# Self-attention's first projections moved into the last groups of cross-attention, in a fused Perceiver layer

## What is computed

```python
def cross(q_in, ctx):                          # x normed, ctx 32 x 256 x 256
    q, k, v = heads16(q_in @ Wq), heads16(ctx @ Wk), heads16(ctx @ Wv)
    return merge(softmax(q @ k.T) @ v) @ Wo
def self_attn(x):                              # x normed
    q, k, v = x @ wq.T, x @ wk.T, x @ wv.T     # per head, 1024 columns in all
    return merge(softmax(causal(q @ k.T / 8)) @ v) @ wo.T
def ffn(x):
    W_in, W_out = quantize_w8(W_in), quantize_w8(W_out)
    h = gelu(quantize_a16(x) @ W_in + b_in)    # a16: scale from the largest |x| of the whole tensor
    return quantize_a16(h) @ W_out + b_out
x = x + cross(norm(x), ctx)
x = x + self_attn(norm(x))
x = x + ffn(norm(x))
```

## Time and profile before

| what | us |
|---|---|
| median of 3 runs | 645.09 |
| their span | 645.08 to 646.16 |
| the profiled execution | 644.6 |
| its span, first to last instruction | 642.9 |
| PE busy | 599.8 (93%) |
| DVE busy | 470.9 (73%) |
| ACT busy | 383.6 (60%) |
| POOL busy | 163.4 (25%) |

### The profile page before, as it was taken

How to read it: one execution, slowest core, us unless ns; L and a number is a source line. 1 busy time by engine, 2 the same in 40 slices (tenths; PEclk the granted TensorE clock), 3 DMA queues, 4 the chain that set the end, 5 groups by cost and what they waited for, 6 DMA issues and landing times. The chain is left out here.

```text
span 642.9 us, 18565 instructions
## 1 busy us (share of the span) xinstructions
PE 599.8 (93%) x6777; PEld 514.1 (80%) x6777; DVE 470.9 (73%) x978; ACT 383.6 (60%) x1012; POOL 163.4 (25%) x229
## 2 busy tenths in 40 slices
PE   6599999999999999889898999999999999799897
PEld 4588888888888898768697989898989898644597
DVE  4478788888888887768799666666666656677797
ACT  3488788888888888756332333333333333457784
POOL 6524233324342423000211212121212111260400
PEclk9899999999999999999999999999999999999999
DMA  6997867686767767814000000000000000000012
GB/s 197 268 259 183 190 162 182 167 191 168 183 171 185 171 162 206 244 54 140 2 2 2 2 0 0 0 0 0 0 0 0 3 1 2 3 2 0 0 50 83
DMA packets 37037, 58.44 MB, mean 91 GB/s; under 512 B 6912, under 2 KB 15232, under 8 KB 36992
## 3 DMA queue, kind: packets, MB, share of 16 engines
q1 hardware_dynamic: 29328, 42.75, 26.2%
q10 hardware_dynamic: 4592, 8.78, 4.7%
q0 software_dynamic: 3072, 6.30, 4.0%
HBM read 17.96 MB, written 2.10 MB: 31 GB/s over the span
## 5 line engine op out<-in xcount | busy, mean ns | idle before, releaser
L624 ACT ACTIVATE Pr<-pS,nmax 128x256 f32<-128x256 f32 x256 | 120.0, 484 | 27.7 <-DVE nmax L732 27.7
L732 DVE TENSOR_REDUCE nmax<-pS 128x2 f32<-128x512 f32 x128 | 87.4, 684 | 20.2 <-PE pS L468 18.6
L478 PE MATMUL pT<-ident,Pr 128*128 128x128 f32 x512 | 78.1, 275 | 3.3 <-DVE wraw L737 3.1
L966 POOL TENSOR_TENSOR a_Pr<-a_Pr,a_rinv 128x512 f32<-128x512 f32 x32 | 32.7, 1043 | 185.8 <-DVE a_rinv L1277 185.8
L468 PE MATMUL pS<-Kst,Qst 96*128 96x256 f32 x256 | 58.9, 312 | 12.1 <-DMA Qst<-QSl 6.8
L1147 ACT ACTIVATE a_Pr<-a_Pr 128x512 f32<-128x512 f32 x32 | 20.2, 631 | 76.0 <-DVE a_Pr L1269 76.0
L478 PEld LDWEIGHTS pT<-ident,Pr 128*128 128x128 f32 x512 | 59.6, 141 | 4.6 <-issue 4.2
L468 PEld LDWEIGHTS pS<-Kst,Qst 96*128 96x128 f32 x256 | 40.2, 193 | 20.9 <-issue 10.0
L624 ACT ACTIVATION_READ_ACCUMULATOR Pr<-pS,nmax 128x1 f32 x256 | 55.0, 215 | 0.0
L287 POOL DMA_DIRECT2D Qst<-QSh x60 | 30.2, 506 | 80.5 <-PE pS L468 56.3
L59 PE MATMUL a_pJ<-a_XTh,a_W1h 128*128 128x256 f32 x128 | 37.1, 290 | 2.5 <-DVE X L1290 1.6
(11 more groups left out here) (323 smaller groups left out, 1974.6 us busy)
## 6 DMA issues: line engine op xcount, KB each, us to landing
Kst<-WO_ints SPq DMA_DIRECT2D x96, 128.0 KB, 3.1
CT<-ctxT ACTq DMA_DIRECT2D x16, 512.0 KB, 4.8
Kst<-KSh SPq DMA_DIRECT2D x62, 128.0 KB, 3.1
Qst<-QSh SPq DMA_DIRECT2D x64, 64.0 KB, 2.3
Qst<-QSh POOLq DMA_DIRECT2D x64, 64.0 KB, 2.9
Kst<-KSl SPq DMA_DIRECT2D x31, 128.0 KB, 3.3
Qst<-QSl SPq DMA_DIRECT2D x32, 64.0 KB, 2.2
Qst<-QSl POOLq DMA_DIRECT2D x32, 64.0 KB, 2.9
```

What stands on the lines that cost most here:

```text
L478: last = pe.transpose(pT[s % 2][:, t, k, :], Pr[s % 2][:, t, P * k:P * k + P], ident[:, :])
L624: act.activation(Pr[c % 2][:, t, :], pS[c % 2][:, t, :], ACT.Exp, bias=nmax[c % 2][:, t:t + 1], accum_out=rsum[par][:, c // 4, 2 * (c % 4) ...
L732: dve.tensor_reduce(nmax[s % 2][:, :], pS[s % 2][:, :, :], AX.X, ALU.max, negate=True).then_inc(maxed, 1)
L966: pool.tensor_tensor(rows, rows, rinv[s][:, :].unsqueeze(2).to_broadcast([P, 8, SQ]), ALU.mult).then_inc(weighted, 1)
```

## The change

- The head of self-attention goes. Quad 0's norm is made in cross-attention's group 6 (steps 4 and 8), its transposes, Q and K in group 7 by the fills of a new table `LAST`: X, the two V fills (now steps 2 and 3), four SQ fills (Q), four SK fills (K), of which the last stands after the group. The filler matmuls at cross-attention's end and in the head go too.
- The weights' splits go from ACT and DVE to POOL (`split_high`, `split_low`, in halves of 128x1024), after its last restack; that of `wo`'s low part (one instruction of 128x2048) to the start of POOL's list in self-attention.
- The split weights, Q and K of quad 0 and all later quads lie in buffers that cross-attention has done with (class `Shared`), K in `raw`. `w_out` gets a buffer of its own; W_in's turned integers and the biases lie in `raw`.
- SP loads `awq` at the end of group 5, `awk` in the middle of group 6.
- Head of cross-attention: the third context load is issued three fills later, and POOL issues the first restack of Q before `rstd_of(1)`.
- The loops over cross-attention's groups and self-attention's quads are written out.
- Feed-forward: the transposes go from block 1 to block 3, their evictions from block 2 to block 4.

```diff
+        self.W = [[cs[0], ks], [qs, cs[1]], [quarter[:2], quarter[2:]]]
+        self.QT = [ct[j // 4][:, 256 * (j % 4):256 * (j % 4) + 256] for j in range(HP)]
+        self.KT = [raw[:, 0, 256 * j:256 * j + 256] for j in range(HP)]
...
+        LAST = {0: ("X", 2, 0), 2: ("V", 1, 0), 3: ("V", 1, 1), 4: ("SQ", 2, 0), 6: ("SQ", 2, 1), 7: ("SQ", 2, 2),
+                8: ("SQ", 2, 3), 10: ("SK", 2, 0), 12: ("SK", 2, 1), 14: ("SK", 2, 2), 16: ("SK", 2, 3)}
...
-            body(0, False)
-            with eng.Fori(1, QUADS - 2) as i:
-                body(i, False)
-            body(QUADS - 2, False)
-            body(QUADS - 1, True)
+            for i in range(QUADS):
+                body(i, i == QUADS - 1)
...
+            def split_high(m):
+                pool.wait_ge(raw_in[m], 16)
+                for k in range(KC):
+                    pool.tensor_copy(shared.W[m][HI][k], raw[:, m, HE * k:HE * k + HE]).then_inc(weights_high, 1)
...
             steps(pool, body)
+            pool.wait_ge(proj, BEFORE_LAST)
+            split_high(0)
+            pool.wait_ge(kst_in[0], RESTACK * QUADS)
+            split_low(0)
+            for par in range(2):
+                q_restacked(pool, par, QUADS)
+            apart(pool, waited)
+            split_high(1)
+            pool.wait_ge(proj, BEFORE_LAST + 3)
+            split_low(1)
+            pool.wait_ge(scores, CHUNKS * (PAIRS - 1))
+            split_high(2)
+            split_low(2)
+            pool.wait_ge(raw_in[3], 16)
+            pool.tensor_copy(shared.WO_high, raw[:, 3, :])
...
+                elif kind in ("SQ", "SK"):
+                    m = ("SQ", "SK").index(kind)
+                    pe.wait_ge(lo, BEFORE_LAST + 1)
+                    pe.wait_ge(weights_split, m + 1)
...
             weigh(QUADS - 1, 12, True)
-            keep_busy(pe, 5, pJ[0][:, :], identb, causal)
+            r, k, kind, ahead, part = event(QUADS - 1, 16, True)
+            project(r, pJ[k % 2], r - 1, kind, part, PAIRS, 0)
             turn_o(PAIRS - 1)
-            keep_busy(pe, 3, pJ[0][:, :], identb, causal)
             turn_back(PAIRS - 1)
-            keep_busy(pe, 5, pJ[0][:, :], identb, causal)
             project_out(PAIRS - 1)
...
-            rstd_of(0)
             rstd_of(1)
+            flat = "p j d -> p (j d)"
+            pool.tensor_tensor(WO[LO].rearrange(flat), raw[:, 3, :], f32(WO[HI]).rearrange(flat), ALU.subtract
+                               ).then_inc(wo_split, 1)
...
-                    if f == 1 and not last:
+                    if f == 3 and not last:
                         turn(g + 1)
```

More of the change, by code:

```diff
@@ L250, in event @@
         def event(i, c, last):
+            if last:
+                if c not in LAST:
+                    return None
+                k = list(LAST).index(c)
+                return BEFORE_LAST + k, k, *LAST[c]
             if c not in EVENTS:
@@ L449, in project @@
                     last = split_matmul(pe, bank[:, :], weights(1, slice(P * part, P * part + P)), parts(CS[b]))
+                elif kind in ("SQ", "SK"):
+                    m = ("SQ", "SK").index(kind)
+                    pe.wait_ge(lo, BEFORE_LAST + 1)
+                    pe.wait_ge(weights_split, m + 1)
+                    for t in range(2):
+                        j = 2 * part + t
+                        last = split_matmul(pe, bank[:, 256 * t:256 * t + 256], shared.weights(m, slice(P * j, P * j + P)),
+                                            parts(XT))
                 else:
@@ L691, in _ @@
             take_even(PAIRS - 1)
+            r, k, kind, ahead, part = event(QUADS - 1, 16, True)
+            high(r, pJ[k % 2], kind, ahead, part, QUADS - 1)
             o_high(PAIRS - 1)
@@ L829, in _ @@
             merge(PAIRS - 1)
+            r, k, kind, ahead, part = event(QUADS - 1, 16, True)
+            low(r, pJ[k % 2], kind, ahead, part, QUADS - 1)
             scale_o(PAIRS - 1)
@@ L994, in bank_read @@
                 if kind == "X":
-                    pe.wait_ge(xt_lo, 2 * quad + part + 1)
+                    pe.wait_ge(xt_lo, 2 * (quad - 1) + part + 1)
                 elif kind == "Y":
@@ L1001, in bank_read @@
                     done, order = (by_act, BY_ACT) if (kind, part) in BY_ACT else (by_dve, BY_DVE)
-                    pe.wait_ge(done, len(order) * quad + order.index((kind, part)) + 1)
+                    pe.wait_ge(done, len(order) * quad + order.index((kind, part)) + 1 - AHEAD)
             def fill(bank, kind, part, quad):
@@ L1047, in score @@
                             rows, side = slice(E * h2, E * h2 + E), (h2 + b) % 2
-                            last = pe.matmul(out[b][SQ * side:SQ * side + SQ, j, :], QT[rows, j, tok],
-                                             KT[rows, j, tok], start=False, stop=True, skip_group_check=True)
+                            last = pe.matmul(out[b][SQ * side:SQ * side + SQ, j, :], QT[j][rows, tok],
+                                             KT[j][rows, tok], start=False, stop=True, skip_group_check=True)
                 last.then_inc(scored, 2)
@@ L1691, in hidden @@
                                       apply_absolute_value=True).then_inc(h_max, 1)
-                    if f == 2 and not last:
+                    if f == 4 and not last:
                         x_low(g + 1)
```

225 lines of the change are left out of this document (111 added, 114 removed).

## The result

| what | before | after |
|---|---|---|
| median of 4 runs, us | 645.62 | 639.73 |
| their span | 645.08 to 646.25 | 635.43 to 641.30 |
| the profiled execution | 644.6 | 641.3 |
| its span | 642.9 | 639.4 |

The ratio is 0.9895, with a 95% interval of 0.9873 to 0.9916: 6 us faster, where 9 were forecast. The profiled execution is one of the two slowest, so its sum comes to -3.5 us of span and not to the median's -5.9.

The account below looks back on a forecast made before the run. PE was taken as nearly full except in group 7, self-attention's head and hidden-stage waits, and DVE as binding quad 0. Terms 0.65 + 5.6 + 1.0 - 18.5 + 4.0 - 1.7 = -8.95 gave median 636.1 us, range 631.5 to 638.8.

Parts of the forecast that it names:

- Group 6, +0.65: Cross-attention's group 6: it now has a norm on DVE, so PE waits at one turn for DVE's copy; +0.65 us.
- Group 7 and the end, +5.6 and +1.0: Cross-attention's last group: nine fills and one X, +5.6 us; at its end the last SK fill's eviction delays On, +1.0.
- The head gone, -18.5: Self-attention's head: after the last addition to X, DVE goes straight to quad 1's statistics; -18.5 us.
- Quad 0's start, +4.0: Self-attention's quad 0: POOL's subtraction for wo blocks DVE's normalise to its end; +4.0 us, with +0.6 and +4.7 as ends.
- Rival 1: Quad 0's start: POOL and DVE pass each other, normalise only stretched or first, +0.7 us instead of +4.0; 632.8 us, 25%.
- The feed-forward, -1.7: Hidden stage: PE's waits for the transposes' input go, a late low part costs a little; -1.7 us, between -1.0 and -2.1.
- The head of cross-attention, 0: Cross-attention's start: first scores 2 to 4 us earlier, lost again waiting for the second K restack; 0, between +0.5 and -2.5.
- The loops, 0: Cross-attention's groups and self-attention's quads: writing out their loops changes no time; 0 us.
- rival 5: Cross-attention: about 29 more packets of PE code come late, each stopping PE; 647.7 us at 0.4 us a packet, 3%.
- Rival 4: Cross-attention's loop: its branch costs the 0.65 us, removal gives 3.2 over five groups, group 6 loses nothing; 632.3 us, 4%.
- Rival 2: Joint of the two attentions: without fillers PE's clock falls to half, losing 1 to 3 us; 638 us, 12%.

## Why the prediction was wrong

Forecast -8.95, measured -3.50 in the profiled execution and -5.9 in the medians. By its own steps:

- *Group 6, +0.65.* +0.36. The norm was costed at the loop's 32.35; written out, such a group takes 32.07. The missing 0.3 is the turn of a loop; the prediction had put the whole 0.65 down to the norm.
- *Group 7 and the end, +5.6 and +1.0.* +6.45 together. Right, and POOL's splits were in time: no wait of PE for them, PE is full (29.00 of 29.00 us from 262.5 on).
- *The head gone, -18.5.* -18.34. Right.
- *Quad 0's start, +4.0.* The mechanism was right, the size was not: the quad lost 5.58, of which the lock, taken away, gives back 5.1. I had taken off 0.7 us for waits that the delay would swallow. It swallowed nothing and added about 0.8, the difference of 5.1 and the 4.25 by which the first maximum was late. PE's second fall to the slow clock stands just there, but no run held the clock up with the lock in place, so that it is the cause is an inference. Rival 1 (632.8 us, 25%) is out.
- *The feed-forward, -1.7.* -2.24 in the trace, -2.5 alone. I had charged 0.1 to 0.2 us for a low part that comes late; it doesn't.
- *The head of cross-attention, 0.* This step failed. "The bytes ahead of it stay the same, so it lands when it landed" was said of the second restack of K, which landed at 40.56 us (41.80 before), and PE did not wait for it. The restack that counted was the first of Q: the third context load had landed before it (20.82 us) and now shares the engines with it. +3.0 in this profile; undoing the load's move alone is worth 3.6 in the medians, undoing both edits 2.4. On the kernel before both edits cost 1.1. I had bounded it by +0.5 on the slow side.
- *The loops, 0.* This step failed too. I looked for the price of code on PE (rival 5: a stop of PE for each packet, 3%) and found none, since PE does not wait for it. The price is paid by ACT and PE, through restacks that land late: +2.7 on the kernel before, 1.6 in groups 1 to 5 of this profile. On the changed kernel the medians say 2.6, within the noise, and the profiles 1.0 in groups 1 to 5. Rival 4's other half is also true, 0.3 us a group, and smaller than the loss. The Trainium skill, "Runtime: NRT & Kernel Launch", "Instruction fetch mechanics", calls the fetch mostly hidden and says that kernels prefer full unrolling where possible; for the engine's own stalls the trace agrees, for the time it doesn't (1.0035).
- *Rival 2, the clock at the joint, 12%.* It fell, and cost some 0.3 us, as DVE was the late one.

The range ended at 638.8, the median is 639.73. Its upper end was built from rival 2; no case had code and context loads as sources of loss, neither one nor both.

## What to carry to other kernels

Before an instruction of POOL on SBUF is put beside a DVE norm or rounding, look which DVE instruction would start second: one wait, that lets the normalise go first, was worth 5 us. Price code and loads not only on the engine that runs them but on the transfers that they share the DMA engines with, above all where a transfer was just in time; a transfer that is neither longer nor earlier issued can still land 3 us later. And before the difference of two medians is put down to an edit, see whether the runs of the two overlap: with four to six runs that lie 4 to 6 us apart, 2.6 us did not come clear of them.

## What the hardware showed that was not expected

- Code is fetched in packets of 16 KB that take 1.1 us of a DMA engine each (61 us for 54). Where one was in flight, a part of a restack took 2.43 to 3.27 us instead of 2.02. Ten instead of one within 120 us of dense restacks go with 2.0 to 2.7 us more, also when only PE's code is longer.
- With the third and fourth context load close together, first scores start at 25.84 to 27.44 us or at 29.36 to 30.28, by whether SP's last low part of Q is issued ahead of the fourth load or behind it.
- POOL's subtraction of 4.6 us blocks DVE's SBUF-to-SBUF normalise to its end, and leaves DVE's reductions and its reads of PSUM at full pace (0.67 to 0.69 us).
- The turn of a hardware loop costs 0.3 us in a group of 32 (32.35 against 32.05), and it still does when only PE's loop is gone (32.35); in self-attention nothing that shows (32.02 and 32.03).
- A granted clock of 0.50 for 6.5 us costs some 0.3 us while DVE is late for other reasons (quad 0 41.49 us against 41.15 with fillers that keep it at 1.00), and the time doesn't move (639.73 against 640.26).
